# A graph-attention and expert layer on one core: edge codes read straight from the staged adjacency, and some logits formed by ScalarE and GpSimd

## The reference, cut to what matters

```python
h = layernorm(x) @ W.T + b_W
e = (h @ a1)[:, None] + (h @ a2)[None, :] + b_a[0]
e = jnp.where(e > 0, e, 0.2 * e)
scores = jnp.where(adj > 0, e, NEG_INF)
x = x + jax.nn.softmax(scores, axis=1) @ h
logits = layernorm(x) @ gate_w + gate_b
# softmax, best two of 16 experts, weights scaled to a sum of one
hidden = silu(x_n @ w1[e]) * (x_n @ w2[e])
x = x + sum_over_two_experts(weight * hidden @ w3[e])
```

## Time and profile before

| | |
|---|---|
| median of three executions | 1613.86 us |
| span of the profiled execution | 1610.0 us |
| median less that span | 3.9 us |
| TensorE busy | 1472.5 us, 91% |
| VectorE busy | 1394.5 us, 87% |
| ScalarE busy | 1283.5 us, 80% |
| GpSimd busy | 553.8 us, 34% |
| blocks 0 / 1 / 2 to 5 | 125.5 / 150.5 / 152.4 us each |
| blocks 6 / 7 / 8 | 149.3 / 144.2 / 80.0 us |
| ahead of block 0 / behind block 8 | 89.7 / 261.0 us |

### The profile page before, as it was taken

The page is one execution under the profiler, slowest core; times in us unless marked ns, Lnnn a source line. Parts: engine busy times, 40 slices in busy tenths (PEclk is TensorE's granted clock), DMA queues, the critical chain, the costliest instruction groups (busy, mean ns, idle before and its releaser), DMA issues.

```text
span 1610.0 us, 25874 instructions
## 1 busy us (share of the span) xinstructions
PE 1472.5 (91%) x8691; PEld 884.2 (55%) x8692; DVE 1394.5 (87%) x1844; ACT 1283.5 (80%) x1662; POOL 553.8 (34%) x791
## 2 busy tenths in 40 slices
PE   4768689999999999999999999999999999999990
PEld 4645245445544554455455445544555556999990
DVE  6889999999999999999999999998889586544444
ACT  4989999999989999999999999997887565433330
POOL 6600000313033503440443236132302435766660
PEclk9999999999999999999999999999999999999995
DMA  7889988778887887788778778882662366889968
GB/s 242 286 304 329 323 276 251 232 221 263 238 246 228 266 252 228 248 258 250 216 245 251 240 212 258 242 239 76 185 168 71 93 152 182 233 269 299 287 196 319
DMA packets 149049, 377.34 MB, mean 234 GB/s; under 512 B 19849, under 2 KB 51785, under 8 KB 148809
## 3 DMA queue, kind: packets, MB, share of 16 engines
q1 hardware_dynamic: 128583, 342.35, 68.5%
q0 software_dynamic: 17152, 27.17, 6.0%
q10 hardware_dynamic: 3202, 6.38, 1.1%
HBM read 347.32 MB, written 32.70 MB: 236 GB/s over the span
## 4 chain that ended last, share of the span: by engine, by line
PE 41%; DVE 31%; issue 14%; POOL 6%; ACT 3%; DMA 3%; SPq 2%; ACTq 0%; POOLq 0%; DVEq 0%
PE pair L1125 22%; DVE ring L1397 15%; DVE probs L1429 13%; PE pair L1227 6%; PE pair L1110 6%; PE pair L1236 3%; ACT ring L870 2%; POOL X L635 1%; DMA ring<-res_d 1%; POOL ln L704 1%; POOL ln L703 1%; PE pair L1220 1%; POOL numT L718 1%; PE pair L1137 1%; ACT probs L921 1%
## 5 line engine op out<-in xcount | busy, mean ns | idle before, releaser
L1125 PE MATMUL pair<-probs,X 128*128 128x512 f32 x2048 | 1009.9, 611 | 1.8 <-ACT probs L921 1.6
L921 ACT ACTIVATE probs<-probs,ebias 128x1024 f32<-128x1024 f32 (+1 forms) x576 | 602.3, 1046 | 124.2 <-DVE probs L1429 121.3
L1429 DVE SCALAR_TENSOR_TENSOR probs<-s1row,ns,pair 128x1024 f32<-128x1024 f32 (+1 forms) x576 | 650.1, 1153 | 48.6 <-PE pair L1110 47.8
L1397 DVE CUSTOM_DVE_ANT_0 ring<-urow,ring 128x2048 int8<-128x2048 f16 x256 | 583.3, 2282 | 5.8 <-ACT urow L889 4.9
L870 ACT ACTIVATE ring<-stage,neghalf 128x1024 int8<-128x1024 int32 x512 | 579.0, 1138 | 0.4 <-DMA stage<-in_adj 0.4
L1110 PEld LDWEIGHTS pair<-diag,ring 128*128 128x128 fp8e5 x4096 | 264.0, 98 | 398.8 <-issue 199.5
L1125 PEld LDWEIGHTS pair<-probs,X 128*128 128x128 f32 x2048 | 346.0, 191 | 219.5 <-issue 215.6
L1110 PE MATMUL pair<-diag,ring 128*128 128x128 bf16 x4096 | 326.1, 220 | 65.1 <-DVE probs L1429 49.9
L767 POOL DMA_INDIRECT xd_d<-xres,sloti x120 | 176.4, 1470 | 39.2 <-issue 31.7
L842 POOL DMA_INDIRECT res_d<-ring x144 | 138.9, 965 | 66.4 <-DVE ring L1835 52.5
L1018 ACT ACTIVATE probs<-pair 128x256 f32<-128x256 f32 x144 | 55.2, 383 | 124.9 <-PE pair L1227 123.1
(11 more groups left out here) (265 smaller groups left out, 665.0 us busy)
## 6 DMA issues: line engine op xcount, KB each, us to landing
stage<-in_adj SPq DMA_DIRECT2D x512, 512.0 KB, 4.4
ring<-w_d SPq DMA_DIRECT2D x144, 256.0 KB, 4.1
ring<-xd_d SPq DMA_DIRECT2D x144, 65.0 KB
ring<-res_d SPq DMA_DIRECT2D x16, 512.0 KB, 9.6
w_d<-in_L_ffn_w SPq DMA_DIRECT2D x32, 128.0 KB, 4.9
out<-ring ACTq DMA_DIRECT2D x8, 512.0 KB, 6.8
ring<-xmid_d SPq DMA_DIRECT2D x1, 3840.0 KB
s1row<-s_d SPq DMA_DIRECT2D x7, 512.0 KB, 6.5
```

Source lines behind the costliest of these rows:

```text
L921: act.activation(probs[:, n % PR, 0:wide], probs[:, n % PR, 0:wide], ACT.Exp, bias=ebias[:, j:j + 1], scale=RISE).then_inc(probs_ready, 1)
L1125: m = pe.matmul(acc[q][:, lo:hi], X[:, j, :], probs[:, n % PR, lo:hi], start=(j == 0), stop=(j == NT - 1))
L1397: dve.tensor_tensor_reduce(m, urow[:, c * CH:(c + 1) * CH], m, CODE, NO_EDGE, ALU.subtract, ALU.max, part[:, k, c:c + 1]).then_inc(piece_d ...
L1429: dve.scalar_tensor_tensor(out=probs[:, n % PR, 0:wide], in0=s1row[:, q, 0:wide], scalar=ns2[:, j:j + 1], in1=Tp[n % 2][:, 0:wide], op0=AL ...
```

## The change

The signs of ScalarE are kept for block 0 and for 20 of the 32 pieces of block 1; all later maxima read the staged int32 adjacency in place of the int8 signs (constants `CODE`, `U_MID`, `U_SPAN` follow from edges being 0 and 1 there). `stage` has 6 slots, that is three pieces, and a slot comes free when the maximum has been taken; the ring holds 44 pieces in place of 48. In 15 units of block 0 and 7 of each full block VectorE forms no logits: ScalarE writes `Relu(row term + neighbour term)` into `probs` (`rise`) and copies the transposed mask to a bf16 tile `gshift` (`shift`), and GpSimd adds the two (`sum_unit`). The layer-norm sums of blocks 0 to 6 move from VectorE's `bn_stats` to ScalarE activations with accumulated output (units 34 to 41). The expert weights' buffers lie in other places of the ring, behind the same waits.

```diff
-CODE = -4.5
-U_MID = 0.11
-U_SPAN = 0.1
+CODE = -9.0
+U_MID = 0.555
+U_SPAN = 0.045
...
-    RING = 6
-    STG = 5
+    RING = 44
+    STG = 6
...
+    GP0 = tuple(51 * (4 * t + 3) // 64 + 5 for t in range(CPT * BLOCKS[1] // 2 - 1))
+    GP = (6, 16, 22, 28, 36, 48, 58)
...
+    SIGNED = PIECE0[1] + 20
+    SIGN_AT = {}
+    for i in range(2 * (SIGNED - PIECE0[1])):
+        SIGN_AT.setdefault(51 * i // (2 * CPT * BLOCKS[1]), []).append(2 * PIECE0[1] + i)
     MAX_AT = [{} for _ in range(NB)]
     for b in range(1, NB):
-        n = 2 * CPT * BLOCKS[b]
+        n = CPT * BLOCKS[b]
         for i in range(n):
-            if 2 <= b and n == NT:
-                j, p = i - 13, i // 2 * 2 - 9
+            if b == 1:
+                p = 51 * (2 * (i | 1) + 1) // (2 * n) + 3
             else:
-                j = 51 * i // n
-                p = j + 3
-            at, j = divmod(NT * (b - 1) + j, NT)
-            SIGN_AT[at].setdefault(j, []).append((b, i))
-            if i % 2:
-                at, p = divmod(NT * (b - 1) + p, NT)
-                MAX_AT[at].setdefault(p, []).append((b, i // 2))
+                p = 2 * i - 9 if 2 * n == NT else 51 * (2 * i + 1) // (2 * n) + 3
+            at, p = divmod(NT * (b - 1) + p, NT)
+            if at >= 1 and p - 1 in gp_units(at):
+                p += 1
+            MAX_AT[at].setdefault(p, []).append((b, i))
...
+                if STG <= n < STG + SIGNS:
                     sp.wait_ge(sign_done, n - STG + 1)
+                elif n >= STG:
+                    sp.wait_ge(piece_done, (n - STG) // 2 + 1)
...
+            def sum_unit(b, j):
+                n = NT * b + j
+                wide = BLOCKS[b] * P
+                pool.wait_ge(piece_done, PIECE0[1] + sum(len(MAX_AT[i].get(u, ())) for i in range(b + 1)
+                                                         for u in range(NT if i < b else j)))
+                pool.wait_ge(rise_ready, gp_before(n + 1))
+                pool.wait_ge(shift_ready, gp_before(n + 1))
+                pool.tensor_tensor(probs[:, n % PR, 0:wide], probs[:, n % PR, 0:wide], gshift[:, 0:wide], ALU.add
+                                   ).then_inc(gsum_ready, 1)
...
+                        if r == 1:
+                            sum_units(b + 1, 18, 31)
...
+                if by_act(b):
+                    pool.wait_ge(rsum_ready, b + 1)
+                    pool.tensor_scalar(r(2), rsum[:, 0, 0:n], -1.0 / D, None, ALU.mult).then_inc(nmean_ready, 1)
+                    pool.wait_ge(squares_ready, b + 1)
+                    plink(pool.tensor_scalar(r(3), rsum[:, 1, 0:n], 1.0 / D, EPS, ALU.mult, ALU.add))
...
+                sum_units(b + 1, 40, 52)
...
             row_end(0)
+            sum_units(0, 0, NT)
             row_end(1)
+            sum_units(1, 0, 8)
...
+                sum_units(b + 1, 8, 18)
                 store_xmid(b)
+                sum_units(b + 1, 31, 40)
...
+                sum_units(b + 1, 52, NT)
                 if b == LAST - 2:
                     prepare()
                 for c in range(2):
                     scatter(b, c)
+                    if c == 0:
+                        sum_units(b + 2, 0, 8)
...
+                if j in gp_units(b):
+                    act.wait_ge(gsum_ready, gp_before(n + 1))
+                    bias = gbias
+                else:
+                    act.wait_ge(logit_ready, dve_before(n + 1))
+                    bias = ebias
+                act.activation(probs[:, n % PR, 0:wide], probs[:, n % PR, 0:wide], ACT.Exp, bias=bias[:, j:j + 1],
                                scale=RISE).then_inc(probs_ready, 1)
+            def rise(b, j):
+                n = NT * b + j
+                q = b % 2
+                wide = BLOCKS[b] * P
+                act.wait_ge(s1_in[q], 16 * (b // 2 + 1))
+                if gp_before(n) == 0:
+                    act.wait_ge(gbias_ready, 1)
+                act.wait_ge(prod_done, n - PR + 1)
+                act.activation(probs[:, n % PR, 0:wide], s1row[:, q, 0:wide], ACT.Relu, bias=scol[:, j, 1:2]
+                               ).then_inc(rise_ready, 1)
+            def shift(b, j):
+                n = NT * b + j
+                wide = BLOCKS[b] * P
+                act.wait_ge(trans_done, n + 1)
+                if gp_before(n) >= 1:
+                    act.wait_ge(gsum_ready, gp_before(n))
+                act.activation(gshift[:, 0:wide], Tp[n % 2][:, 0:wide], ACT.Copy).then_inc(shift_ready, 1)
...
+            def row_sums(b, k):
+                if k % 4 == 0:
+                    act.wait_ge(xadd_in[k // 4], 16 * added(b, k // 4))
+                ins = act.activation(acc[b % 2][:, k * D:(k + 1) * D], xres[:, b % 2, k, 0:D], ACT.Copy,
+                                     accum_out=rsum[:, 0, k:k + 1])
+                if k == BLOCKS[b] - 1:
+                    ins.then_inc(rsum_ready, 1)
+            def row_squares(b, k):
+                if k == 0:
+                    act.wait_ge(nmean_ready, b + 1)
+                ins = act.activation(acc[b % 2][:, k * D:(k + 1) * D], xres[:, b % 2, k, 0:D], ACT.Square,
+                                     bias=ln2[:, 2, k:k + 1], accum_out=rsum[:, 1, k:k + 1])
+                if k == BLOCKS[b] - 1:
+                    ins.then_inc(squares_ready, 1)
...
+                    if j + 2 in gp_units(b):
+                        rise(b, j + 2)
                     exps(b, j)
-                    for of, i in SIGN_AT[b].get(j, ()):
-                        sign(of, i)
+                    if b == 0:
+                        for n in SIGN_AT.get(j, ()):
+                            sign(n)
+                    if j + 2 in gp_units(b):
+                        shift(b, j + 2)
...
+                        for i in (0, 1):
+                            k = 2 * (j - SUMS_AT) + i
+                            if 0 <= k < BLOCKS[b - 1]:
+                                row_sums(b - 1, k)
+                            k = 2 * (j - SQUARES_AT) + i
+                            if 0 <= k < BLOCKS[b - 1]:
+                                row_squares(b - 1, k)
...
-                    pe.wait_ge(logit_ready, n - 1)
+                    if (n - 2) % NT in gp_units((n - 2) // NT):
+                        pe.wait_ge(shift_ready, gp_before(n - 1))
+                    else:
+                        pe.wait_ge(logit_ready, dve_before(n - 1))
...
-                dve.wait_ge(sign_done, 2 * (PIECE0[b] + i + 1))
-                dve.tensor_tensor_reduce(m, urow[:, c * CH:(c + 1) * CH], m, CODE, NO_EDGE,
+                if PIECE0[b] + i < SIGNED:
+                    dve.wait_ge(sign_done, 2 * (PIECE0[b] + i + 1))
+                    edges = m
+                else:
+                    n = 2 * (PIECE0[b] + i)
+                    for half in (n, n + 1):
+                        dve.wait_ge(adj_in[half % STG], 16 * (half // STG + 1))
+                    before = PIECE0[b] + i - RING
+                    if before == 0 or before > 0 and (i == 0 or group_of(before) > group_of(before - 1)):
+                        dve.wait_ge(trans_done, used_up(group_of(before)))
+                    edges = stage[:, n % STG:n % STG + 2, :].rearrange("p a b -> p (a b)")
+                dve.tensor_tensor_reduce(m, urow[:, c * CH:(c + 1) * CH], edges, CODE, NO_EDGE,
                                          ALU.subtract, ALU.max, part[:, k, c:c + 1]).then_inc(piece_done, 1)
...
-                    logits(b, j)
+                    if j not in gp_units(b):
+                        logits(b, j)```

VectorE in units 14 to 21 of block 2, before. L1429 is `logits`, the two ISA rows are `maxima` and the read of its accumulator.

```order
L1429 SCALAR_TENSOR_TENSOR probs<-s1row,ns,pair 128x1024 x2
L1397 ISA ring,part<-urow,ring 128x2048
L1397 ISA part 128x1
L1429 SCALAR_TENSOR_TENSOR probs<-s1row,ns,pair 128x1024 x2
L1397 ISA ring,part<-urow,ring 128x2048
L1397 ISA part 128x1
```

129 lines of the change are left out of this document (78 added, 51 removed).

## The result

The kernel after takes 1620.16 us (median of four runs, 1619.13 to 1621.53) against 1613.92 us for the kernel before in runs beside it: 1.0038 times as long, with an interval of 1.0026 to 1.0050. It is 0.4% slower, where 1594 us and faster was predicted. The profiled execution has a span of 1617.4 us.

What follows compares the result with a forecast made beforehand. VectorE sets the pace in blocks 2 to 5, TensorE's floor is 144.2 us. Savings 18.4 + 3.5 + 2.6 less 2.0 and 3.0 make 19.5 us: 1610.0 - 19.5 + 3.9 = 1594 us; own range 1578 to 1606, whole 1572 to 1619.

Steps and rivals of the forecast that it cites:

- The int32 operand: VectorE's maxima reading staged int32: claimed to stay at 2.21 us, bounded by that and a tenth more.
- GpSimd's sum: GpSimd's addition for handed-over units: claimed 2.40 us for 1024 elements, 1.29 us for 512.
- ScalarE's saving is worth nothing: Full blocks: ScalarE falls from 144.5 us to well under 110, claimed worth nothing since nobody waited for signs.
- VectorE loses 10.1 us a block: Full blocks: VectorE loses seven `logits`, 8.4 us, and statistics, 1.7 us, going from 152.4 to 142.3 us.
- The floor by quarters: Full blocks: the larger of VectorE's and TensorE's time in each quarter, TensorE at 36.05 us each, sums to 145.3 us.
- The new waits: Full blocks: late work at units 6, 46 and 58, together 4.5 us, partly absorbed; taken as 2.5 us a block.
- Block 7: Block 7, already at TensorE's floor: claimed to take the late sums and get 2.0 us longer.
- Block 0: Block 0: ScalarE's first half 73.4 us, then VectorE's remaining work; 128.4 us against 125.5, 3 us longer.
- The sums lock out the maxima: Rival, blocks 1 to 6: late GpSimd sums hold VectorE's maxima, +42 us, 1636 us; chance 0.14.
- The gate logits come later: Rival, seven blocks: gate logits later than 1.5 us by 2 us more, 1608 us; chance 0.11.
- The adjacency: Rival: maxima wait for staged adjacency loads, +3 to +12 us in block 0, about 1602 us; chance 0.12.
- The floor: Rival: all new waits hide, blocks 1 to 7 at TensorE's 144.2 us, block 0 as before, 1570 us; chance 0.13.

Runs made afterwards that it cites:

- direct_only: Changed kernel without handed-over units, single maxima in block 0, squares without the mean in units 34 to 37: 0.9948 of the kernel before, 1672.1 us.
- quiet_gp: Changed kernel with only units 16, 22, 28 and 36 of a full block handed over; 6, 48, 58 back on VectorE: 1.0004 of the kernel before.
- best_c: Changed kernel, block 0 without pairs or handed-over units, squares early without mean, unit 50 for 48, sums 6 and 58 earlier: 0.9883 of before, 1660.6 us.
- b0_singles: Changed kernel with block 0's maxima one at a time in place of pairs, its 15 handed-over units kept: 1.0046 of the kernel before.
- no_gp: Changed kernel with no handed-over units anywhere; pairs of maxima and ScalarE's sums stay: 1.0033 of the kernel before.
- b0_plain: Changed kernel without block 0's 15 handed-over units and with its maxima one at a time: 0.9974 of the kernel before, 1671.1 us.
- norm_early: Changed kernel with squares taken without the mean in units 34 to 37, variance formed on GpSimd: 1.0010 of the kernel before, 1614.6 us.

## Why the prediction was wrong

The sign was wrong, and the time by 26 us. By the spans the forecast missed by 26.9 us: 14.8 in blocks 2 to 5 together, 7.5 in block 0, 2.1 in block 6, 0.6 in block 1 and 2.4 in block 8 and behind it, less 0.5 that block 7 lost less than I said. Step by step:

- **The int32 operand** was right: the unheld maximum takes 2.28 us on `stage` as on the `ring`, and none waited for a load.
- **GpSimd's sum** was right in size: 2.13 and 1.16 us against 2.40 and 1.29.
- **ScalarE's saving is worth nothing**: right, `direct_only` shows it.
- **VectorE loses 10.1 us a block**: too much by 2.6. Its busy time fell by 7.5 us, from 152.1 to 144.6. In block 3 the two held maxima (3.10 and 2.82 us for 2.28 each) are 1.4 us of that; the other 1.2 us I did not trace.
- **The floor by quarters** is the first step that failed. I spread TensorE's time evenly, 36.05 us a quarter; block 7 of before has 36.5, 36.5, 35.5 and 35.4. With the first two at 36.5 the sum is 146.2 in place of 145.3 us, and the units handed over in the second quarter can earn only 0.3 us, as `quiet_gp` shows. The larger of two engines over a quarter is also too kind in the last one: predicted 37.0, it is 38.8 us in `best_c`, where no sum is late. VectorE's work there comes in lumps, as its timeline ahead of unit 53 shows, and its lead is at most two halves of `Tp`. No run took the lumps out, so their price is not measured.
- **The new waits, "I take 2.5 us, between 0 and 5"** failed in size, and it is the largest term of the full blocks. I listed units 6, 46 and 58, which came, at 0.5, 0.6 and 1.1 us beyond a quiet step, where I had 1.5 to 2, 1.5 and 1.3. I missed unit 48, the costliest: the step of 4.54 us, 2.3 more than 2.21. I had not priced GpSimd's own wait for VectorE's choice (3.48 us) with a sum queued behind it, of which 1.7 us came on top of the sum's wait for its maximum. That the four add up to 4.5 us, the "together 4.5" of the prediction, is luck; what I took as absorbed, 2.0 of them, was not. In block 3 the 145.3 us, 0.9 more of floor and 4.5 of waits make 150.7 of the 151.2 measured. Blocks 2 to 5 took 151.5 us on average in place of 147.8 (they saved 0.9 us each, not 4.6), block 6 saved 0.5 in place of 2.6, and block 1, without the routing of a full block behind it, 2.9 of 3.5.
- **Block 7** lost 1.5 us, predicted 2.0.
- **Block 0, "3.0 more"**, failed by 7.5 us, the largest miss in one block. The first half came out right (73.4 predicted, 72.4 measured), but by luck. I had added up ScalarE's work alone. With the handed-over units alone (`b0_singles`) it takes 78.8 us, since ScalarE also waits 7.2 us for sums that maxima hold, a term I put at nothing. With the pairs alone (`no_gp`), where ScalarE has no `rise` or `shift`, it still takes 73.1 us. In the second half I let VectorE be three units ahead, with its maximum behind unit 34, and do 2.2 + 52.8 us after that; it took 64.5. VectorE had no such lead: before, it was busy for 63.2 us there, six narrow `logits` less leave 59.2, and it was busy for 60.2. The rest is waiting for transposes, 4.8 us in that half. I had costed two maxima as twice one; first half and second together, `no_gp` shows that the pairs alone cost 8.5 us over `b0_plain`.

**The rivals.** *The sums lock out the maxima* is true as a mechanism and not as a price. On 205 maxima of the full blocks the mean is 2324 ns against 2283 unheld: 8.4 us in all, 0.17 us for each of 49 sums, below the 0.46 from which it would decide. In block 0 the mean of the 20 on the `ring` is 2538 ns, 5 us in all (16 of the 36 in the group above lie ahead of it). Held are the maxima beside sums that were late for another reason: in `best_c` seven sums a block, on time, hold none in the full blocks. By the Trainium skill (SBUF — State Buffer, Who interferes with whom) the shared ports go to whichever started first; the trace now agrees in both directions (a maximum of 3.10 us behind a running sum, a step of 2.25 us behind a running maximum). *The gate logits come later*: about 1 us a block, as `norm_early` and the 1.1 us between `no_gp` and `direct_only` show. *The adjacency* did not come late: DMA moves 278 GB/s in the first half of block 0 against 322 before, but no maximum waited for a load, and with `b0_plain` it is 324 again. *The floor* was not reached.

**What stays open**: the 2.4 us in block 8 and behind it; the 1.2 us of VectorE's busy time; how the costs of the pairs and of the handed-over units share block 0 when both are there, since its time differs by 5.4 us between executions; and that the parts of `best_c` were not each taken out of it alone.

## What to carry to other kernels

Work moved to an engine that is idle on average is worth something only if that engine's program order lets it start on time: before handing a step over, look for what is queued ahead of it there and what that waits for, since the in-order queue of the next engine passes the delay on to everything behind. Take floors and leads at the scale of the buffers between the engines (here two units, 4.4 us), not at that of a quarter or a block, and count the work that comes in pieces longer than that. When a change has several parts and is slower, take each part alone: here the sums on ScalarE, started earlier, are worth 8 us, and the handed-over units, with two sums moved and unit 50 for 48, another 12 us. As first placed, the sums on ScalarE were worth nothing and the handed-over units 0.5 us in each of blocks 2 to 5, and block 0 cost some 10 us on top.

## What the runs showed of the hardware

- A tensor-tensor of GpSimd on 128 x 1024 took 2.13 us and on 128 x 512 1.16 us, so 1.9 ns an element between them, below the 2.17 ns that 64 and 128 elements gave. The second operand is bf16 here.
- A running sum of GpSimd lengthened VectorE's maximum from 2.28 to 3.10, 2.82 and (in block 0) up to 3.24 us; a running maximum lengthened an operation of GpSimd from 0.20 to 2.25 us, and the narrow sums in the first half of block 0 from 1.16 to 2.3 us on average (`b0_singles`). A routing step of VectorE beside a moved sum took 2.12 us in place of 0.29. Each time the one that started first kept its own duration.
- ScalarE's accumulating activation on 128 x 128 costs two instructions: 262 ns and an accumulator read of 188 ns, which overlap by about 0.06 us.
- VectorE's maximum reads int32 from `stage` at the same 2.28 us as int8 from the `ring`.
